# Joining the edge blocks of three attention passes in five parts instead of one

## The chip, the cores and the metric

One NeuronCore of a Trainium2 chip runs the whole kernel. The metric is the device time of one execution in microseconds (us), the median of the runs shown.

## The reference, cut to what matters

A stack of four graph layers on N = 3125 nodes and E = 50000 edges with 128 features: a GCN layer, an edge-attention layer with 8 heads ("attn"), two GAT layers with 3 heads and 1 head ("gat1", "gat2"), and two SAGE layers. The change touches the three attention layers only. Each computes, per head and per destination node,

```python
m = segment_max(logits, dst)
ex = exp(logits - m[dst])
denom = segment_sum(ex, dst)
agg = segment_sum(ex / denom[dst] * rows[src], dst)
```

## The kernel before, in words

The edges are sorted by destination and cut into CH = 392 blocks of 128 edges; GC = 4 blocks are a group (NG = 98), two groups a pair (NPR = 49). An attention pass (`edge_pass`, one function on each engine) walks over the groups with a hand-written software pipeline: `ticks` calls a list of stages once per pair, each with its own lag, so the order inside a list is the order in that engine's queue.

Per group, POOL gathers the source rows with 4 indirect DMAs (L1021) into a ring of RB = 8 slots; before group n it waits for the message multiply of group n-8 (`msg_done`). SP loads the same-destination masks, the breaks and, in attn, the edge attributes and destination rows, each into a ring of four. PE turns attributes (`attr_t`, L1565), multiplies them into edge terms (`edge_terms`, L1573), spreads destination rows over the edges (`dst_rows`, L1584 in attn, L1589 in the GAT passes) and sums the messages per destination (`sums`, L1613). DVE does, in this order per pair: `maxima` (two scans, L2257 and L2263, which need PE's transpose of the logits), `terms` of the even group (attn: L2224 adds the edge terms, L2227 multiplies, L2243 reduces; GAT: L2234, L2247), `difs` (L2270, needs PE's `max_t`, L1604), `terms` of the odd group, and `messages` (L2286) of the two groups before. ACT copies PSUM out (`evac`, L1052), takes the exponentials (L1189) and stores every block's sums to the scratch tensor `ends` (L1167).

Edge terms and destination rows go to two PSUM banks each, by turns, so PE may compute those of group g+1 while DVE still reads those of group g:

```python
                    if g >= 2:
                        pe.wait_ge(kve_done.sem, kve_done.at(p, g, 2))
                    for k in range(GC):
                        i = mm(bank((1, 6)[g % 2])[:, k * D:(k + 1) * D], at_t[:, g % 2, k * P:(k + 1) * P], w_e[:, :],
```

A node's edges can run over a block's edge, so after the last group the blocks are joined: a scan over all 392 blocks for the running maximum, four factors (exponentials of differences), and for the denominators and every 128 columns a scan of the sums. This is the tail of a pass: PE L1626 brings the blocks' maxima together, DVE L2300 to L2316 and ACT L1221 make the factors, PE L1642 spreads them over the partitions, L1659 turns the first and last rows of the blocks (which SP loads back from `ends` by L631), DVE L2328 to L2335 scan, PE L1671 turns back, ACT copies, SP stores (L631), and only then POOL gathers the results (L1030) for the node-wise stage that follows. The tail's chain is serial: each step waits for the one before.

Of the kernel before, what the change touches and what calls it, by code (L numbers as in the profile page):

```python
# [9 lines left out]
ALU = mybir.AluOpType  # L10
# [62 lines left out]
def groups_by(b):  # L73

    return max(0, b - SAME0) * NG // (NB - SAME0)

# [100 lines left out]
def gnn_stack_kernel(nc, out, x, src, dst, edge_attr_64, **w):  # L177
    ctx = ExitStack()
    with ctx:
# [150 lines left out]
        r_rows = place(9700, CQ, QA, wide_w)  # L330
        z_rows = place(11748, CQ, QA, wide_w)
        f_rows = place(13296, CQ, QA, wide_w)
        ex_sb = place(14844, P, 4, CH)
        u_col = place(16412, P, CH)
        s_col = place(16804, P, CH)
        t_col = place(17196, P, H2, CH)
        ex_h = place(18372, H1, 4, CH)
        run_m = place(19940, H1, CH)
        top_m = place(20332, H1, CH)
        u_den = place(20724, H1, CH)  # L340
        s_den = place(21116, H1, CH)
        t_den = place(21508, H1, CH)
# [128 lines left out]
        spread_ps = sem("spread_ps")  # L471
        col_ps, col_ex, col_done, col_back, col_out = (sem(f"col_{k}") for k in ("ps", "ex", "done", "back", "out"))
# [51 lines left out]
        for p in ("gcn",) + PASSES + ("sage1", "sage2"):  # L524
            if p in WEIGHTED:
                chain("s_" + p, ["firsts"] + (["er_in", "er_ps", "er_sb"] if p != "attn" else []))
                chain("x_" + p, ["z_in", "r_out"])
# [71 lines left out]
        cols_of, at_cols = {}, 0  # L599
        for p in PASSES:  # L600
            cols_of[p] = at_cols
            at_cols += col_chunks(p) + 1

        def col_at(p, ch):

            return cols_of[p] + ch + 1

        SPAN_STEPS = 5
        span_of, at_span = {}, 0
        for p in PASSES:  # L610
            span_of[p] = at_span + SPAN_STEPS
            at_span += SPAN_STEPS + 3 * (col_chunks(p) + 1)

        def span_end(p):

            return span_of[p]
# [10 lines left out]
        def _(sp):  # L627
# [151 lines left out]
            def edge_pass(p):  # L779
                c = chains["x_" + p]  # L780
# [39 lines left out]

                for g in range(NG):
# [3 lines left out]
                for g in (NG - 2, NG - 1):  # L825
                    sp.wait_ge(ends_out.of(g), ends_out.at(p, g))
                sp.wait_ge(s_steps, c.at("z_in"))
                v = ends[p][0:EP, :].rearrange("(a t e) c -> t a e c", a=QA, e=P)
                load(z_rows[:, :, 0:W], v[:, :, 0, :])
                load(f_rows[:, :, 0:W], v[:, :, P - 1, :])  # L830
                landed()
                sp.sem_inc(s_steps, 1)
                sp.wait_ge(col_out, col_at(p, col_chunks(p)))
                load(ends[p][EP + P:EP + P + CH, :].rearrange("(a t) c -> t a c", a=QA), r_rows[:, :, 0:W])
                landed()
                sp.sem_inc(s_steps, 1)
# [26 lines left out]
            sp.wait_ge(s_steps, chains["x_gat2"].end)  # L863
# [12 lines left out]
        def _(pool):  # L876
# [130 lines left out]
            def edge_pass(p):  # L1007
# [18 lines left out]
                pool.wait_ge(s_steps, chains["x_" + p].end)  # L1026
# [21 lines left out]
        def _(act):  # L1048
# [111 lines left out]
            def edge_pass(p):  # L1160
# [45 lines left out]

                if p in er_all:
# [5 lines left out]
                if p == "attn":  # L1213
                    ticks([(evac, 2, -4), (keep_max, 1, -1), (attr_sb, 2, 2), (exps, 1, -1), (evac, 2, -3),
                           (attr_sb, 2, 3), (same_f32, 2, 3), (same_f32, 2, 4), (store_ends, 2, -4), (store_ends, 2, -3)])
                else:
                    ticks([(evac, 2, -4), (keep_max, 1, -1), (exps, 1, -1), (evac, 2, -3),
                           (same_f32, 2, 3), (same_f32, 2, 4), (store_ends, 2, -4), (store_ends, 2, -3)])

# [1354 lines left out]
```

## Time and profile before

| | us |
|---|---|
| median of 3 runs (3553.38 to 3568.37) | 3554.34 |
| profiled execution, its own time | 3551.71 |
| its span | 3550.1 |

The page gives PE busy 69% of the span, PE's weight loads 52%, DVE 40%, ACT 27%, POOL 38%; the granted TensorE clock is 0.743 on the mean. The three passes stand in the trace at about 715 to 1444 us (attn), 1571 to 2312 us (gat1) and 2420 to 3128 us (gat2), 98 groups each. No engine is busy all the time, so shares do not tell the bound: it has to be read from who waits for whom.

### The profile page before, as it was taken

Reading aid. Unit: us, or ns where it says so; the run is one execution under the profiler, and the core shown is the slowest. Engines: PE = TensorE matmul, PEld = TensorE weight load, DVE = VectorE, ACT = ScalarE, POOL = GpSimd, SP = SyncE. Lnnn points to the kernel's source line nnn. Section 1 sums busy time; section 2 is a strip of 40 time slices with the busy share of each in tenths; the row PEclk is TensorE's granted clock in tenths of the full one; section 3 lists DMA queues with packets and bytes.
Section 4 is the critical chain, followed back from the end, with each engine's and each line's share of the span. In section 5 each row is a group of like instructions: output and inputs, shape, how many; then the busy total and the mean of one; then the engine's idle time right before and its main releaser. Section 6 shows DMA issues by size and latency. Waiting matters only on the chain.

```text
span 3550.1 us, 36582 instructions
## 1 busy us (share of the span) xinstructions
PE 2464.1 (69%) x12427; PEld 1828.4 (52%) x12427; DVE 1418.4 (40%) x3070; ACT 962.5 (27%) x2050; POOL 1354.0 (38%) x1417
## 2 busy tenths in 40 slices
PE   4999997377666766545677666664565655649998
PEld 3666665256555555333444444443564555526666
DVE  6756555244444455533333333431221212251423
ACT  3422223122222222442333333231221222220202
POOL 3000002645444553375555555045565555320000
PEclk9777788677777787667888888776555555569999
DMA  9388641456666674124555655322344444346362
GB/s 210 115 300 297 234 147 39 139 167 189 175 177 180 177 199 142 26 55 125 169 184 172 189 181 186 107 70 52 88 112 95 106 105 103 94 137 205 116 205 66
DMA packets 518595, 517.78 MB, mean 146 GB/s; under 512 B 154128, under 2 KB 463763, under 8 KB 517227
## 3 DMA queue, kind: packets, MB, share of 16 engines
q1 hardware_dynamic: 310349, 267.24, 24.9%
q0 software_dynamic: 50528, 115.22, 13.3%
q10 hardware_dynamic: 157534, 132.98, 11.9%
q8 instruction: 102, 1.67, 0.2%
q14 instruction: 82, 0.67, 0.1%
HBM read 301.13 MB, written 227.33 MB: 149 GB/s over the span
## 4 chain that ended last, share of the span: by engine, by line
PE 40%; another core or an unknown queue 25%; DVE 12%; issue 12%; ACT 6%; DMA 2%; POOL 1%; ACTq 0%; DVEq 0%; SPq 0%
PE ps L1613 9%; PE ps L1540 8%; PE ps L1434 6%; PE ps L1444 5%; ACT arena L1052 4%; DVE arena L2224 2%; DMA ends_gat<-arena 1%; PE ps L1522 1%; DVE arena L2286 1%; PE ps L1589 1%; PE ps L1573 1%; PE ps L1584 1%; DVE arena L1934 1%; DVE arena L2227 1%
## 5 line engine op out<-in xcount | busy, mean ns | idle before, releaser
L1052 ACT ACTIVATE arena<-ps 128x544 f32<-128x544 f32 (+9 forms) x591 | 485.9, 825 | 1746.1 <-remote 874.5
L1613 PE MATMUL ps<-arena 128*128 128x136 f32 (+2 forms) x2352 | 695.9, 460 | 376.3 <-ACT arena L1052 194.6
L1021 POOL DMA_INDIRECT arena<-t_gat,src_i x784 | 741.9, 946 | 537.1 <-DVE arena L2286 307.8
L1613 PEld LDWEIGHTS ps<-arena 128*128 128x128 f32 x2352 | 479.6, 269 | 516.4 <-issue 425.2
L1021 POOL DMA_INDIRECT arena<-t_attn,src_i x392 | 375.4, 958 | 344.1 <-DVE arena L2286 225.3
L2257 DVE TENSOR_TENSOR_SCAN arena<-arena,ps 64x128 f32<-64x128 f32 (+2 forms) x147 | 60.0, 408 | 803.0 <-remote 714.2
L1540 PE MATMUL ps<-arena 128*128 128x384 bf16 x1850 | 308.2, 331 | 37.6 <-issue 25.1
L1589 PEld LDWEIGHTS ps<-arena 128*128 128x128 f32 x1568 | 288.3, 268 | 45.2 <-issue 22.5
L1589 PE MATMUL ps<-arena 128*128 128x3 f32 (+1 forms) x1568 | 266.6, 292 | 15.7 <-issue 15.7
L1540 PEld LDWEIGHTS ps<-arena 128*128 128x128 bf16 x1850 | 183.1, 99 | 162.4 <-issue 46.0
L2286 DVE TENSOR_TENSOR arena<-arena,ps 128x1536 f32<-128x1536 f32 (+1 forms) x196 | 230.6, 1218 | 38.7 <-ACT arena L1189 30.1
L1444 PE MATMUL ps<-arena 128*128 128x100 bf16 x1176 | 224.4, 364 | 9.4 <-DVE arena L2064 9.2
L1434 PE MATMUL ps<-arena 128*128 128x385 bf16 x925 | 221.0, 413 | 0.0
L984 POOL TENSOR_TENSOR arena<-arena,r_L_gnn_gamma 128x512 f32<-128x512 f32 (+1 forms) x7 | 8.1, 1158 | 533.4 <-ACT arena L1252 533.3
L1444 PEld LDWEIGHTS ps<-arena 128*128 128x128 bf16 x1176 | 169.3, 145 | 58.9 <-DVE arena L2064 12.6
L1573 PE MATMUL ps<-w_e,arena 64*128 64x128 f32 x784 | 148.6, 324 | 59.7 <-issue 59.2
L1604 PE MATMUL ps<-ident,arena 64*128 64x64 f32 (+2 forms) x147 | 40.8, 278 | 201.1 <-DVE arena L2263 164.9
L2270 DVE TENSOR_TENSOR dif<-logit,ps 128x64 f32<-128x64 f32 (+2 forms) x147 | 27.4, 187 | 374.9 <-remote 199.5
L1052 ACT ACTIVATE arena<-same_b 128x512 f32<-128x512 bf16 x294 | 167.7, 619 | 29.6 <-DMA same_b<-same_hbm 28.7
L1573 PEld LDWEIGHTS ps<-w_e,arena 64*128 64x128 f32 x784 | 120.4, 222 | 88.5 <-issue 88.4
L1434 PEld LDWEIGHTS ps<-arena 128*128 128x128 bf16 x925 | 112.2, 121 | 102.9 <-issue 68.9
L1052 ACT ACTIVATE arena<-arena 128x512 bf16<-128x512 f32 (+4 forms) x208 | 64.3, 309 | 346.1 <-DVE arena L2524 247.8
(320 smaller groups left out, 2942.1 us busy)
## 6 DMA issues: line engine op xcount, KB each, us to landing
ends_gat<-arena ACTq DMA_DIRECT2D x98, 774.0 KB
arena<-adj_hbm SPq DMA_DIRECT2D x90, 640.0 KB, 4.2
same_b<-same_hbm SPq DMA_DIRECT2D x294, 128.0 KB
adj_hbm<-arena SPq DMA_DIRECT2D x9, 3200.0 KB, 11.8
ends_attn<-arena ACTq DMA_DIRECT2D x98, 272.0 KB
ends_gat<-arena ACTq DMA_DIRECT2D x98, 258.0 KB
arena<-edst SPq DMA_DIRECT2D x98, 256.0 KB, 4.2
starts_q<-zrow SPq DMA_DIRECT2D x28, 896.0 KB, 6.8
```

The source lines that it names most:

```text
L1021: g.indirect_dma_start(out=row_b[:, n % RB, k, 0:row_tab[p].shape[1]], out_offset=None, in_=row_tab[p], in_offset=bass.IndirectOffsetOnAxi ...
L1052: return a.activation(o, i, ACT.Copy)
L1434: i = mm(bank(4 + n % 4)[:, 0:3 * D + 1], lhs, xs0[:, t, 0:3 * D + 1], start=t == 0, stop=t == NT - 1)
L1444: i = mm(ps[:, at:at + KEYS], hot_e[:, b % 3, :, e], hot_k[:, b % 3, :, e], start=True, stop=True)
L1540: m = mm(bank(ch % 2 * 4 + dl)[:, 0:3 * D], ring[:, u % RING, at:at + P], xs1[:, t, :, :].rearrange("p s c -> p (s c)"), start=t == 0, sto ...
L1573: i = mm(bank((1, 6)[g % 2])[:, k * D:(k + 1) * D], at_t[:, g % 2, k * P:(k + 1) * P], w_e[:, :], start=True, stop=True)
L1589: i = mm(ps[:, at:at + n_er], same_f[:, g % RB, k, :], er_c[:, g * GC + k, 0:n_er], start=True, stop=True)
L1604: nc.tensor.transpose(bank(2)[:, 256:256 + kh], mx[0:kh, i % 2, :], ident[0:kh, 0:kh])\
L1613: i = mm(o, same_f[:, g % RB, k, :], msg[:, g % 4, k * W:(k + 1) * W], start=True, stop=True)
L2224: tt(kv, kv, bc(bank((1, 6)[g % 2]).rearrange("p (k s c) -> p k s c", k=GC, s=1), [P, GC, 2, D]), ALU.add).then_inc(kve_done.sem, 1)
L2257: v.tensor_tensor_scan(fwd[0:kh, s, :], b[:, 0:P], bank(2)[0:kh, 0:P][:, ::-1], -BIG, ALU.add, ALU.max)\
L2286: tt(m[:, :, 0:heads * nc_].rearrange("p k (h c) -> p k h c", h=heads), rows_v, e, ALU.mult).then_inc(msg_done.sem, 1)
```

## The change

The 392 blocks are split in five parts, the first four of 72 blocks (18 groups) and the last of 104. Each of the first four is joined inside the pass, by small steps ("mini") that are put in the tick lists some 7 to 20 groups after the part's last group; the running maximum and the scanned sums are carried from part to part. The last part alone is joined after the last group, by the same chain as before over 104 blocks. `slots_of` fixes at which group's slot each step stands; in a slot of an even group DVE's step comes before `messages`, in one of an odd group after them. Buffers: the part's rows, factors and scans lie in other places of the arena and in a node-stage buffer. A PSUM bank is needed for a part while the groups go on: bank 6 in attn and gat2, bank 1 in gat1. For that, attn's edge terms have bank 1 alone, and gat1's destination rows bank 3 alone; gat2 keeps both of its banks. The `wait` for DVE's use of them goes back one group instead of two. In PE's lists of attn and gat1 `max_t` moves before `edge_terms` and `dst_rows`.

On DVE `tops` is 9 small operations, `mask` is 1 and `join` 7 per chunk of columns, on 72 to 105 columns each. On PE `edges_of` is 16 small products, and it calls `cols_in`, which waits for the two row loads that SP issued (`s_rows`). Not shown of the diff: the semaphore counts and the steps' own waits.

```diff
+PARTS = [(0, 72), (72, 144), (144, 216), (216, 288), (288, CH)]
...
+        def slots_of(p):
...
+            for q in range(QP - 1):
+                s = PARTS[q][1] // GC + 7
+                put(s, "edges", q, 0)
+                put(s + 1, "tops", q, 0)
+                put(s + 2, "exp", q, 0)
+                put(s + 3, "mask", q, 0)
+                put(s + 3, "join", q, 0)
+                for ch in range(1, col_chunks(p) + 1):
+                    put(s + 1 + 3 * ch, "cols", q, ch)
+                    put(s + 2 + 3 * ch, "copy", q, ch)
+                    put(s + 3 + 3 * ch, "join", q, ch)
+                s += 4 + 3 * col_chunks(p)
+                put(s, "back", q, 0)
+                put(s + 1, "rows", q, 0)
...
@@ SP, edge_pass @@
+                def rows_for(q):
+                    b0, b1 = PARTS[q]
+                    g1 = b1 // GC
+                    for g in (g1 - 2, g1 - 1):
+                        sp.wait_ge(ends_out.of(g), ends_out.at(p, g))
+                    if part_at(p, q) > 1:
+                        sp.wait_ge(col_ps, col_at(p, q, 0) - 1)
+                    sp.dma_start(z_rows[0:b1 - b0, 0:W], v_ends[b0:b1, 0, :]).then_inc(s_rows, 16)
+                    sp.dma_start(f_rows[0:b1 - b0, 0:W], v_ends[b0:b1, P - 1, :]).then_inc(s_rows, 16)
...
+                def sums_out(q):
+                    b0, b1 = PARTS[q]
+                    sp.wait_ge(col_out, back_at(p, q, col_chunks(p)))
+                    sp.dma_start(ends[p][EP + P + b0:EP + P + b1, :], r_rows[0:b1 - b0, 0:W]).then_inc(s_rout, 16)
...
+                rows_at = {PARTS[q][1] // GC + 10: q for q in range(QP - 1)}
+                out_at = {PARTS[q][1] // GC + 19 + 3 * col_chunks(p): q for q in range(QP - 1)}
                 for g in range(NG):
                     if g % 2 == 0:
                         load_breaks(g // 2)
                     load_group(g)
+                    if g in out_at:
+                        sums_out(out_at[g])
+                    if g in rows_at:
+                        rows_for(rows_at[g])
...
@@ ACT, edge_pass, gat1 and gat2 (attn the same with attr_sb) @@
+                    ticks([(evac, 2, -4), (keep_max, 1, -1), (exps, 1, -1), (mini, 2, 0), (evac, 2, -3),
+                           (same_f32, 2, 3), (same_f32, 2, 4), (store_ends, 2, -4), (store_ends, 2, -3),
+                           (mini, 2, 1)])
...
@@ PE, edge_pass @@
                 def edge_terms(g):
                     pe.wait_ge(attr_sb_done.sem, attr_sb_done.at(p, g))
-                    if g >= 2:
-                        pe.wait_ge(kve_done.sem, kve_done.at(p, g, 2))
+                    if g >= 1:
+                        pe.wait_ge(kve_done.sem, kve_done.at(p, g, 1))
                     for k in range(GC):
-                        i = mm(bank((1, 6)[g % 2])[:, k * D:(k + 1) * D], at_t[:, g % 2, k * P:(k + 1) * P], w_e[:, :],
+                        i = mm(bank(1)[:, k * D:(k + 1) * D], at_t[:, g % 2, k * P:(k + 1) * P], w_e[:, :],
...
                 def dst_rows(g):
                     pe.wait_ge(same_f_done.sem, same_f_done.at(p, g))
-                    if g >= 2:
-                        pe.wait_ge(prod_done.sem, prod_done.at(p, g, 2))
+                    back = 1 if p == "gat1" else 2
+                    if g >= back:
+                        pe.wait_ge(prod_done.sem, prod_done.at(p, g, back))
...
-                            at = (3, 1)[g % 2] * BANK + k * n_er
+                            at = (3, 3 if p == "gat1" else 1)[g % 2] * BANK + k * n_er
...
+                def edges_of(q, ch=0):
+                    b0, b1 = PARTS[q]
+                    i0, i1 = b0 // PB, b1 // PB
+                    pe.wait_ge(kept_done.sem, kept_done.at(p, i1 - 1))
...
+                    for s, t in enumerate((o.last[:, 1:], o.first)):
+                        for k in range(PB):
+                            i = mm(t[:, k::PB], ident[0:kh, k * heads:(k + 1) * heads], edge_m[0:kh, i0:i1, s],
+                                   start=True, stop=True)
+                    i.then_inc(edge_m_ps, 1)
+                    if q < QP - 1:
+                        cols_in(q, 0)
...
                 if p == "attn":
-                    ticks([(logit_t, 1, -1), (sums, 2, -4), (attr_t, 2, 2), (edge_terms, 2, 1), (dst_rows, 2, 1),
-                           (max_t, 1, -1), (sums, 2, -3), (attr_t, 2, 3), (edge_terms, 2, 2), (dst_rows, 2, 2)])
+                    ticks([(logit_t, 1, -1), (sums, 2, -4), (attr_t, 2, 2), (max_t, 1, -1), (edge_terms, 2, 1),
+                           (dst_rows, 2, 1), (sums, 2, -3), (attr_t, 2, 3), (mini, 2, 0), (edge_terms, 2, 2),
+                           (dst_rows, 2, 2), (mini, 2, 1)])
+                elif p == "gat2":
+                    ticks([(logit_t, 1, -1), (sums, 2, -4), (dst_rows, 2, 1), (max_t, 1, -1), (sums, 2, -3),
+                           (mini, 2, 0), (dst_rows, 2, 2), (mini, 2, 1)])
                 else:
-                    ticks([(logit_t, 1, -1), (sums, 2, -4), (dst_rows, 2, 1), (max_t, 1, -1), (sums, 2, -3),
-                           (dst_rows, 2, 2)])
-
+                    ticks([(logit_t, 1, -1), (sums, 2, -4), (max_t, 1, -1), (dst_rows, 2, 1), (sums, 2, -3),
+                           (mini, 2, 0), (dst_rows, 2, 2), (mini, 2, 1)])
...
@@ DVE, edge_pass @@
-                ticks([(maxima, 1, -1), (terms, 2, 0), (difs, 1, -1), (terms, 2, 1), (messages, 2, -2), (messages, 2, -1)])
+                ticks([(maxima, 1, -1), (terms, 2, 0), (difs, 1, -1), (terms, 2, 1), (mini, 2, 0), (messages, 2, -2),
+                       (messages, 2, -1), (mini, 2, 1)])
+                tops(QP - 1)
+                mask(QP - 1)
                 for ch in range(col_chunks(p) + 1):
+                    join(QP - 1, ch)
```

## Rows read from the trace of the kernel before

**Rows 1.** Busy time by stretch, the three passes' loops; then PEclk, DMA share, GB/s.
```profile
715.00:1415.00 700.00, 493.53 (x2766) 413.11 (x2765) 346.26 (x528) 180.22 (x429) 345.01 (x360) 0.75 0.63 176
1571.00:2269.00 698.00, 441.05 (x1680) 287.50 (x1681) 240.65 (x441) 216.42 (x393) 371.45 (x393) 0.81 0.54 167
2420.00:3099.00 679.00, 372.96 (x1709) 359.97 (x1710) 141.13 (x466) 136.50 (x394) 382.35 (x404) 0.51 0.41 97
```
**Rows 2.** Waits, attn's loop, then gat1's: us in total, times, longest.
```profile
POOL arena L1021 <- DVE arena L2286: 225.3, 27, 20.0
...
POOL arena L1021 <- DVE arena L2286: 165.7, 51, 10.6
```
**Rows 3.** Timeline of POOL in attn: end of one run of gathers, start of the next.
```profile
1009.77 0.95 POOL L1021 DMA_INDIRECT arena<-t_attn,src_i  x1 [0.30 <-issue]
1021.50 0.94 POOL L1021 DMA_INDIRECT arena<-t_attn,src_i  x1 [10.78 <-DVE arena L2286]
```
**Rows 4.** Timeline of attn between those two: DVE and PE.
```profile
1013.71 2.07 PE L1584 MATMUL ps<-arena 128*128 128x128 f32 x8 [0.34 <-issue]
...
1013.86 0.41 DVE L2257 TENSOR_TENSOR_SCAN arena<-arena,ps 64x128 f32<-64x128 f32 x1 [14.63 <-remote]
...
1014.65 1.19 DVE L2224 TENSOR_TENSOR arena<-arena,ps 128x1024 f32<-128x1024 f32 x1
...
1017.48 1.22 DVE L2224 TENSOR_TENSOR arena<-arena,ps 128x1024 f32<-128x1024 f32 x1
...
1018.71 1.16 PE L1573 MATMUL ps<-w_e,arena 64*128 64x128 f32 x8
...
1019.79 1.16 PE L1584 MATMUL ps<-arena 128*128 128x128 f32 x8
```
**Rows 5.** Busy time by stretch, the same place: columns as in Rows 1.
```profile
1013.80:1018.30 4.50, 4.50 (x19) 4.07 (x20) 4.26 (x7) 1.74 (x6) 0.00 (x0) 0.50 0.64 179
1018.50:1032.00 13.50, 10.34 (x78) 8.81 (x76) 9.98 (x16) 3.93 (x10) 8.07 (x9) 1.00 0.73 208
```
**Rows 6.** Timeline of gat1 at such a place.
```profile
1836.40 0.41 DVE L2257 TENSOR_TENSOR_SCAN arena<-arena,ps 24x128 f32<-24x128 f32 x1 [11.49 <-remote]
...
1837.70 0.17 DVE L2234 TENSOR_TENSOR z_b<-arena,ps 128x12 f32<-128x12 f32 x1
...
1840.90 0.95 POOL L1021 DMA_INDIRECT arena<-t_gat,src_i  x1 [7.20 <-DVE arena L2286]
...
1842.21 0.95 PE L1589 MATMUL ps<-arena 128*128 128x3 f32 x8
```
**Rows 7.** Timeline of gat2 at such a place: DVE, then POOL.
```profile
2569.00 0.41 DVE L2257 TENSOR_TENSOR_SCAN arena<-arena,ps 8x128 f32<-8x128 f32 x1 [15.12 <-remote]
...
2572.29 0.94 POOL L1021 DMA_INDIRECT arena<-t_gat,src_i  x1 [6.35 <-DVE arena L2286]
```
**Rows 8.** Timeline of attn's tail: its first step, SP's store, the gather that follows.
```profile
1414.94 2.78 PE L1626 MATMUL ps<-arena,ident 64*8 64x49 f32 x32
...
1441.08 0.31 SPq L631 DMA_DIRECT2D ends_attn<-arena  x1
1443.90 0.95 POOL L1030 DMA_INDIRECT arena<-ends_attn,end_i  x1 [63.74 <-SPq L836]
```
**Rows 9.** Groups by form in attn's tail: busy us, mean ns.
```profile
L2331 DVE TENSOR_TENSOR_SCAN arena<-arena 128x392 f32<-128x392 f32 x1 | 1.0, 974 | 0.0
...
L2306 DVE COPY arena<-span_m 8x1 f32<-8x1 f32 x1 | 0.1, 131 | 0.0
```
**Rows 10.** Chain of gat1's tail, its first step and its end; then gat2's.
```profile
2269.00 1.54 PE ps L1626 x32
...
2307.98 3.75 DMA ends_gat<-arena
2311.77 0.26 issue
...
3099.63 2.71 PE ps L1626 x32
...
3128.51 0.94 POOL arena L1030
```

More of the change, by code:

```diff
@@ L75, in groups_by @@
     return max(0, b - SAME0) * NG // (NB - SAME0)
+PARTS = [(0, 72), (72, 144), (144, 216), (216, 288), (288, CH)]
+QP = len(PARTS)
+PW = max(b - a for a, b in PARTS)
+assert all(a % PB == 0 for a, b in PARTS) and PW <= P
 PIECE = [(c, t, t + HI) for c in range(NC - 1) for t in range(0, NT, HI)] + [(NC - 1, 0, 13), (NC - 1, 13, NT)]
@@ L824, in edge_pass @@
                     load_group(g)
[L825 to L836, printed above, removed]
+                    if g in out_at:
+                        sums_out(out_at[g])
+                    if g in rows_at:
+                        rows_for(rows_at[g])
+                for q in range(QP - 1):
+                    if PARTS[q][1] // GC + 19 + 3 * col_chunks(p) >= NG:
+                        sums_out(q)
+                rows_for(QP - 1)
+                sums_out(QP - 1)
             for j in range(NJ):
@@ new lines, in spread_of @@
+                def spread_of(q, ch):
+                    n = PARTS[q][1] - PARTS[q][0]
+                    if ch == 1:
+                        pe.wait_ge(span_dve, span_at(p, q) + SPAN_STEPS)
+                        if q == QP - 1:
+                            pe.wait_ge(evac_done.sem, evac_done.at(p, NG - 1))
+                    elif q == QP - 1:
+                        pe.wait_ge(col_ex, ex_at(p, q, ch) - 1)
+                    for e in range(4):
+                        lhs = spread[:, :] if p == "attn" else bc(ident[0:heads, ch - 1:ch], [heads, P])
+                        i = mm(Psum(p, q).ex[e], lhs, ex_h[0:heads, e, 0:n + 1], start=True, stop=True)
+                    i.then_inc(spread_ps, 1)
@@ new lines, in cols_in @@
+                def cols_in(q, ch):
+                    n = PARTS[q][1] - PARTS[q][0]
+                    o = Psum(p, q)
+                    if ch == 0:
+                        if q == QP - 1:
+                            pe.wait_ge(span_set, part_at(p, q))
+                        pe.wait_ge(s_rows, 32 * part_at(p, q))
+                    elif ch >= 2 or q < QP - 1:
+                        pe.wait_ge(col_done, col_at(p, q, ch - 1))
+                    for t, z in ((z_rows, o.den_z if ch == 0 else o.z), (f_rows, o.den_f if ch == 0 else o.f)):
+                        if ch == 0:
+                            src_v = t[0:n, heads * cols:W]
+                        elif p == "attn":
+                            src_v = t[0:n, 0:heads * cols]
+                        else:
+                            src_v = t[0:n, (ch - 1) * cols:ch * cols]
+                        i = nc.tensor.transpose(z, src_v, ident[0:n, 0:n])
+                    i.then_inc(col_ps, 1)
+                    if 0 < ch and q < QP - 1:
+                        spread_of(q, ch)
```

356 lines of the change are left out of this document (207 added, 149 removed).

## The prediction

> **What bounds the kernel now.** I read first the busy time by stretch for the three loops [rows 1]. Each takes 679 to 700 us for 98 groups, and no engine is busy throughout: PE 441 and POOL 371 of 698 us in gat1, PE 494 and POOL 345 of 700 us in attn. So the loops are bound by handing over, not by an engine, and the waits have to say whose. In attn POOL waited 225.3 us in 27 waits for the message multiply L2286; in gat1 165.7 us, in more and shorter waits [rows 2]. POOL's timeline shows the form: gathers come in runs, most of 16 (four groups), one every 1.25 us, so 20 us a run; after the run that ended at 1010.7 POOL idled 10.78 us and began again at 1021.50 [rows 3]. What ends that pause is read on DVE: it sat idle 14.63 us, resumed with the scan L2257 at 1013.86, and POOL began again 7.6 us later, when the tick's messages were out [rows 4]. In gat1 the resume is at 1836.40 and POOL's start at 1840.90, 4.5 us later, after a pause of 7.20 [rows 6]; in gat2 2569.00, 2572.29, 3.3 us and 6.35 [rows 7]. The pause less that stretch is 3.1, 2.7 and 3.1 us: the same in all three. So a period is a run of gathers (20 us), a lag of about 3 us, and then **the stretch from DVE's resume to the first messages**. What holds DVE until the run is over the rows don't say (the wait has no releaser in them), but whatever is done during the run is free, and whatever lengthens the stretch after it is paid in every period. 98 groups by four make 24.5 periods; some are shorter or overlap, so I count 225.3 / 10.8 = 21 for attn and 165.7 / 7.2 = 23 for gat1.
>
> **Part 1, the tails.** From PE's first join step to POOL's first gather, attn's tail takes 1443.90 - 1414.94 = 29.0 us [rows 8], gat1's 2311.77 + 0.26 - 2269.00 = 43.0, gat2's 3128.51 - 3099.63 = 28.9 [rows 10]. All of it is on the path, since POOL gathers the results only after it. After the change the chain is the same over 104 blocks instead of 392. What doesn't shrink: SP's store to the gather's start, 2.8 us in attn [rows 8], 4.1 in gat1 [rows 10]; and the fixed part of each operation, 0.13 us by a copy of one column [rows 9], about 30 operations in attn and 45 in gat1, so 4 and 6 us; and 1 to 2 us of handing over. The rest scales with 104/392 = 0.27: a scan falls from 0.974 us [rows 9] to about 0.36 (0.41 for 128 columns [rows 4]). Attn: 29.0 - 2.8 - 4 - 1 = 21.2, to 5.7, so 13.5 are left and 15.5 saved. Gat2 the same. Gat1: 43.0 - 4.1 - 6 - 2 = 31, to 8.4, so 20.5 left and 22.5 saved. In attn and gat2 SP's rows of the last part come about when the shorter chain wants them, so I take 1 us off: **52 us saved**, bounds 40 (fixed costs twice as large) and 58. The price of PE's 32 tiny products in it (13 columns instead of 49) is the least certain; by the rows it is between 0.27 of 2.78 us [rows 8] and all of it, and I took 0.27 of the variable part. The Trainium skill, TensorE: Matmul & The Clock Gate, Part 1, says start to start never drops below about 25 ns however few the columns; by that estimate the 32 would take at least 0.8 us a pass. No row here has 13 columns.
>
> **Part 2, attn's edge terms in one bank.** Now PE makes edge terms and destination rows of the odd group during the stall: its L1584 ends about when DVE resumes [rows 4], so DVE goes from the even group's L2224 (1014.65, 1.19 us) over two multiplies and `difs` straight to the odd group's L2224 at 1017.48. After the change `edge_terms` of the odd group must wait for the even group's L2224, that is until 1015.85, and destination rows stand behind it in PE's queue. Two prices for these 16 matmul instructions: 1.16 + 1.16 us as at 1018.71 and 1019.79, or twice 2.07 as L1584 at 1013.71 [rows 4]. With 0.15 us for the semaphore the odd L2224 begins at 1018.3 (+0.8) or 1020.1 (+2.7). The granted clock decides: it was 0.50 (1.2 GHz) from 1013.8 to 1018.3, after the stall, and 1.00 (2.4 GHz) from 1018.5 on [rows 5]. So the first falls wholly and the second mostly on 1.2 GHz: I take +2.0 us. Queued behind PE's new wait are `sums` and the even group's work; behind DVE's are the messages, POOL's restart and so the next run. In the tick inside the run the same wait falls at 2.4 GHz, where `difs` waited for `max_t` anyway, and `max_t` now comes earlier: nothing. 21 x 2.0 = **+42 us**, bounds 0 (if the period gives way elsewhere) and 24.5 x 2.7 = 66.
>
> The Trainium skill, same page, Part 1, says that the throttled clock is the default and activity releases it; by that rule PE, left waiting longer in the stall, comes back at the low clock, and the term would be 21 x 2.7 = 57 rather than the 17 of the high clock. The trace agrees as far as 0.50 after the stall [rows 5] goes.
>
> **Part 3, gat1's destination rows in one bank.** The same, smaller. Now the odd L2234 runs at 1837.70, 1.3 us after the resume; after the change its 8 products (0.95 us at 1842.21 [rows 6]; about 1.7 by attn's ratio of 2.07 to 1.16 [rows 4]) start only after the even L2234 and `max_t`, which end at about 1837.6. So it begins at 1838.7 to 1839.4, +1.0 to +1.7. DVE waited there for the exponentials before the messages, which takes 0.3 of it back: I take +1.0. 23 x 1.0 = **+23 us**, bounds 0 and 24.5 x 1.4 = 34.
>
> **Part 4, the steps inside the passes.** PE (16 products, transposes, spreads), ACT (an exponential, copies) and SP (three small DMAs a part) have room during the stalls; none of theirs stands between resume and messages in their queues. DVE's do when their slot is even: at 0.2 us an operation (between 0.13 [rows 9] and 0.41 [rows 4]) `tops` 1.8 and `mask` with the first `join` 1.6 us, in gat1 one more `join` 1.4. Each meets the stretch that counts in one tick of two: 4 parts x 3.4 / 2 = 7 us in attn and gat2, 4 x 4.8 / 2 = 10 in gat1: 24 us. Some of it falls where DVE waits: **+20 us**, bounds 8 and 35. If the stalls' cover went, it would be about 80 us of PE, ACT and DVE work more. SP's new waits come after its loads for the group, four groups ahead of use, and I cost them at nothing.
>
> **The sum.** -52 + 42 + 23 + 20 = +33 us against the profiled execution's own 3551.7 us, which is 2.6 below the median of 3554.3; on the median, **3587 us**. About 0.5% (18 us) is what a measurement of this kernel can tell from no change.
>
> **Rivals.**
> A, the tails come off and the loops don't notice: the wait moves into the 14 us of stall, because the tick in which the run ends shifts so that PE's new wait falls inside the run. For it: the stall is long and POOL's restart needs only one tick. Against it: three passes with stretches of 7.6, 4.5 and 3.3 us have the same 3 us of lag, so the stretch is paid in full each time. It gives 3554 - 52 + 12 = 3514 us. Chance 0.27.
> B, in between: the high clock after the stall, or half of the periods hit: -52 + 17 + 12 + 20 = -3, 3551 us. Chance 0.13.
> C, slower by another wait: PE's `edges` slot calls `cols_in`, which waits for rows that SP asks for in the same pair or the pair before; if they land only when the run of gathers is over, PE stands before the next logit transposes, and POOL's next run starts a tick late. 12 parts at up to 7.6 us [rows 4] are 91 us on top of nothing else lost: 3554 - 52 + 33 + 91 = 3626 us. It decides from the point where a row load takes longer than one tick, about 7 us. Chance 0.10, beside 0.50 for my forecast.
> D, the change doesn't do what it says: the last part's chain is no shorter, because the rows that SP loads after the last store set its pace. The store, the load and their landing are some 7 us, the shorter chain up to that point about 6: it costs 1 to 2 us a pass and is in the bounds.
>
> **Range and chances.** A has faster; B lies within 0.5%; the forecast and C are slower, though the forecast's lower fifth isn't by over 0.5%. Faster 0.28, same 0.16, slower 0.56. The range takes in A with its costs, 3508, and reaches up to the forecast's upper bounds short of all at once, 3640. The forecast's own range is 3560 to 3640.
>
> **What would show it.** The tails at about 14, 21 and 14 us; in attn the odd L2224 after a resume some 5 us after the even one instead of 2.8, with L1573 and L1584 between them; POOL's pauses 12 to 13 us in attn, 8 in gat1, unchanged in gat2 but for some; runs still of 16. Wrong if attn's loop stays at 700 us, or if a row wait (`s_rows`) stands in PE's list.

## The result, and the profile after

The changed kernel takes 3619.73 us (median of 4 runs, 3600.88 to 3624.94) where the kernel before took 3556.52 on the same chip: ratio 1.017, 95% interval 1.0136 to 1.0204, that is +60 us (48 to 73). Forecast were +33 us, 3587, with a range to 3640. The profiled execution has a span of 3623.0 us.

The page of the changed kernel: the span, three engines, then the gathers and the messages.

```profile
span 3623.0 us, 38294 instructions
...
PE 2501.5 (69%) x12995; PEld 1875.2 (52%) x12995; DVE 1455.3 (40%) x3430; ACT 965.6 (27%) x2106; POOL 1347.4 (37%) x1417
...
L1109 POOL DMA_INDIRECT arena<-t_gat,src_i x784 | 740.0, 944 | 593.1 <-DVE arena L2419 364.2
...
L1109 POOL DMA_INDIRECT arena<-t_attn,src_i x392 | 371.4, 947 | 421.8 <-DVE arena L2419 303.8
```

PE is as busy as before, 69%. What grew is POOL's wait for the message multiply (now L2419), in attn from 225.3 us [rows 2] to 303.8. POOL's timeline tells where: it gives a pass three marks, its first gather of rows, its last, and the first gather of results. Before:

```profile
660.97 0.98 POOL L1021 DMA_INDIRECT arena<-t_attn,src_i  x1 [0.30 <-issue]
1379.20 0.95 POOL L1021 DMA_INDIRECT arena<-t_attn,src_i  x1 [0.30 <-issue]
1571.68 0.97 POOL L1021 DMA_INDIRECT arena<-t_gat,src_i  x1 [0.30 <-issue]
2222.16 0.94 POOL L1021 DMA_INDIRECT arena<-t_gat,src_i  x1 [0.30 <-issue]
2445.17 0.97 POOL L1021 DMA_INDIRECT arena<-t_gat,src_i  x1 [0.31 <-issue]
3071.22 0.94 POOL L1021 DMA_INDIRECT arena<-t_gat,src_i  x1 [0.30 <-issue]
```

After, the same with the gather of results (L1118):

```profile
662.86 0.97 POOL L1109 DMA_INDIRECT arena<-t_attn,src_i  x1 [0.30 <-issue]
1454.62 1.05 POOL L1109 DMA_INDIRECT arena<-t_attn,src_i  x1 [0.30 <-issue]
1503.73 0.94 POOL L1118 DMA_INDIRECT arena<-ends_attn,end_i  x1 [48.06 <-DMA ends_attn<-arena]
1630.62 0.97 POOL L1109 DMA_INDIRECT arena<-t_gat,src_i  x1 [0.30 <-issue]
2321.96 0.95 POOL L1109 DMA_INDIRECT arena<-t_gat,src_i  x1 [0.30 <-issue]
2388.72 0.94 POOL L1118 DMA_INDIRECT arena<-ends_gat,end_i  x1 [65.82 <-DMA ends_gat<-arena]
2520.90 0.97 POOL L1109 DMA_INDIRECT arena<-t_gat,src_i  x1 [0.30 <-issue]
3160.13 0.95 POOL L1109 DMA_INDIRECT arena<-t_gat,src_i  x1 [0.30 <-issue]
3203.67 1.00 POOL L1118 DMA_INDIRECT arena<-ends_gat,end_i  x1 [42.59 <-DMA ends_gat<-arena]
```

From the first gather of rows to the last ("the loop" from here on) the passes take 718, 650 and 626 us before, 792, 691 and 639 after: +74, +41, +13, in sum +128. From the last gather of rows to the gather of results ("the tail") it is 64.7, 89.9 and 57.3 before [rows 8, 10 give the ends], 49.1, 66.8 and 43.5 after: -53 together. 128 - 53 = 75, and the two profiled spans are 73 us apart, so little else moved. (By the medians it is +60; the profiled execution is the longest of the four.) The joins did leave the tails, and by as much as forecast. What went wrong is in the loops, forecast at +85.

The tail of attn itself, with the rows that answer to [rows 8], and the first step of gat2's tail:

```profile
1490.95 0.96 PE L1734 MATMUL ps<-arena,ident 64*8 64x13 f32 x32
...
1501.90 0.30 SPq L908 DMA_DIRECT2D ends_attn<-arena  x1
1503.73 0.94 POOL L1118 DMA_INDIRECT arena<-ends_attn,end_i  x1 [48.06 <-DMA ends_attn<-arena]
...
3190.35 0.95 PE L1734 MATMUL ps<-arena,ident 8*1 8x13 f32 x32
```

From PE's first step to POOL's gather attn's tail takes 12.8 us, where 13.5 stood in the sum; the 32 records of the tiny products took 0.96 us. (A product of this kernel stands in the trace as two records: x32 is 16 products.)

**How the loops changed.** In attn, runs of 16 gathers turned into runs of 8 for most of the pass. (Here and below a pause of under 2 us doesn't end a run. Of the 360 gathers behind the first 32, 32 stood in runs of 8 before and 216 after.) The timeline of attn, one such period:

```profile
1010.43 0.94 POOL L1109 DMA_INDIRECT arena<-t_attn,src_i  x1 [5.83 <-DVE arena L2419]
...
1012.87 1.19 DVE L2357 TENSOR_TENSOR arena<-arena,ps 128x1024 f32<-128x1024 f32 x1
...
1014.81 1.30 PE L1681 MATMUL ps<-w_e,arena 64*128 64x128 f32 x8
...
1019.18 0.95 POOL L1109 DMA_INDIRECT arena<-t_attn,src_i  x1 [0.30 <-issue]
1021.92 1.22 DVE L2357 TENSOR_TENSOR arena<-arena,ps 128x1024 f32<-128x1024 f32 x1 [6.29 <-remote]
...
1023.29 2.04 PE L1681 MATMUL ps<-w_e,arena 64*128 64x128 f32 x8 [4.72 <-DVE arena L2357]
...
1025.93 0.94 POOL L1109 DMA_INDIRECT arena<-t_attn,src_i  x1 [5.81 <-DVE arena L2419]
```

The even group's L2357 (the addition of the edge terms, L2224 before) runs at 1012.87. PE's edge terms of the odd group (L1681) had to wait for it and stand in PE's list at 1014.81, 4.4 us into the run of gathers, but the odd L2357, which needs them, starts only at 1021.92, 2.7 us after the last gather was issued. In the kernel before they stand 0.9 us into the run:

```profile
990.91 0.94 POOL L1021 DMA_INDIRECT arena<-t_attn,src_i  x1 [10.47 <-DVE arena L2286]
...
991.78 1.16 PE L1573 MATMUL ps<-w_e,arena 64*128 64x128 f32 x8
...
995.37 1.22 DVE L2224 TENSOR_TENSOR arena<-arena,ps 128x1024 f32<-128x1024 f32 x1
```

The odd L2224 follows at 995.37, within the run, the whole second tick gets through, and 16 gathers are freed. Now a period is 15.5 us for 8 gathers, 31.0 for 16 instead of 30.55, and where a run of 16 still occurs it mostly takes 32 to 37 us. The slower pace is more than the 0.45 us between 31.0 and 30.55: on the mean of the loop behind its first 32 gathers, 16 of them took 29.3 us before and 32.5 after.

In gat2, whose banks are untouched, all but four of the periods are like before (24.9 to 26.5 us for 16 gathers). One of those that are not:

```profile
2832.20 0.94 POOL L1109 DMA_INDIRECT arena<-t_gat,src_i  x1 [6.42 <-DVE arena L2419]
...
2833.53 0.95 PE L1734 MATMUL ps<-arena,ident 8*1 8x9 f32 x32
2834.41 0.40 PE L1769 MATMUL ps<-ident,arena 72*1 72x72 f32 x2
2834.60 0.42 PE L1706 MATMUL ps<-ident,logit 128*8 128x128 f32 x1
...
2840.95 0.94 POOL L1109 DMA_INDIRECT arena<-t_gat,src_i  x1 [0.30 <-issue]
2842.19 0.41 DVE L2390 TENSOR_TENSOR_SCAN arena<-arena,ps 8x128 f32<-8x128 f32 x1 [10.15 <-issue]
```

Here a part's `edges` (L1734) stands ahead of the logit transpose L1706, which the scan L2390 needs. By the records it all fits into 1.1 us, yet the scan that needs L1706 starts 7.2 us after the end of it, when the run, 8 gathers long now, is over; 15.4 us for 8 gathers instead of 13. In gat1 one part shows more of it:

```profile
1961.48 0.69 PE L1734 MATMUL ps<-arena,ident 24*3 24x9 f32 x22
1963.19 0.22 PE L1734 MATMUL ps<-arena,ident 24*3 24x9 f32 x3 [1.01 <-issue]
1963.91 0.17 PE L1734 MATMUL ps<-arena,ident 24*3 24x9 f32 x1 [0.49 <-issue]
1965.33 0.17 PE L1734 MATMUL ps<-arena,ident 24*3 24x9 f32 x1 [1.25 <-issue]
...
1973.06 0.40 PE L1769 MATMUL ps<-ident,arena 72*3 72x72 f32 x2 [1.23 <-issue]
```

The first 22 records go in 0.7 us and the last ten take about 10: PE waits for nothing that the profile shows and mostly advances by one record in 0.7 us or a multiple of it, while POOL gathers.

### The profile page after: what moved, and what is told of

It reads as the page before. It is cut to its first block and busy times, and to the rows that moved or that the text cites. A ratio compares the mean times of both kernels' runs of the same rounds, so it can differ in the third digit from the quotient of the medians.

```text
span 3623.0 us, 38294 instructions
## 1 busy us (share of the span) xinstructions
PE 2501.5 (69%) x12995; PEld 1875.2 (52%) x12995; DVE 1455.3 (40%) x3430; ACT 965.6 (27%) x2106; POOL 1347.4 (37%) x1417
## 3 DMA queue, kind: packets, MB, share of 16 engines
q0 software_dynamic: 50528, 115.22, 12.8%
## 5 line engine op out<-in xcount | busy, mean ns | idle before, releaser
L1140 ACT ACTIVATE arena<-ps 128x544 f32<-128x544 f32 (+7 forms) x610 | 479.2, 794 | 1893.7 <-remote 882.5
L1722 PEld LDWEIGHTS ps<-arena 128*128 128x128 f32 x2352 | 486.3, 271 | 367.8 <-issue 290.7
L1109 POOL DMA_INDIRECT arena<-t_attn,src_i x392 | 371.4, 947 | 421.8 <-DVE arena L2419 303.8
L2390 DVE TENSOR_TENSOR_SCAN arena<-arena,ps 64x128 f32<-64x128 f32 (+2 forms) x147 | 60.0, 408 | 776.8 <-remote 635.7
L1698 PEld LDWEIGHTS ps<-arena 128*128 128x128 f32 x1568 | 292.7, 275 | 61.8 <-issue 52.1
L1698 PE MATMUL ps<-arena 128*128 128x3 f32 (+1 forms) x1568 | 282.4, 302 | 43.6 <-issue 20.6
L1681 PE MATMUL ps<-w_e,arena 64*128 64x128 f32 x784 | 150.8, 349 | 185.9 <-DVE arena L2357 168.0
L2419 DVE TENSOR_TENSOR arena<-arena,ps 128x1536 f32<-128x1536 f32 (+1 forms) x196 | 230.1, 1215 | 17.5 <-ACT arena L1277 11.9
L1681 PEld LDWEIGHTS ps<-w_e,arena 64*128 64x128 f32 x784 | 131.5, 251 | 202.0 <-ACT arena L1140 117.3
L2357 DVE TENSOR_TENSOR arena<-arena,ps 128x1024 f32<-128x1024 f32 x98 | 118.0, 1204 | 265.4 <-remote 219.1
L1713 PEld LDWEIGHTS ps<-ident,arena 64*128 64x128 f32 (+2 forms) x147 | 23.2, 158 | 358.9 <-DVE arena L2396 302.3
```

Of the source, the lines that this page charges most:

```text
L1109: g.indirect_dma_start(out=row_b[:, n % RB, k, 0:row_tab[p].shape[1]], out_offset=None, in_=row_tab[p], in_offset=bass.IndirectOffsetOnAxi ...
L1140: return a.activation(o, i, ACT.Copy)
L1681: i = mm(bank(1)[:, k * D:(k + 1) * D], at_t[:, g % 2, k * P:(k + 1) * P], w_e[:, :], start=True, stop=True)
L1698: i = mm(ps[:, at:at + n_er], same_f[:, g % RB, k, :], er_c[:, g * GC + k, 0:n_er], start=True, stop=True)
L1713: nc.tensor.transpose(bank(2)[:, 256:256 + kh], mx[0:kh, i % 2, :], ident[0:kh, 0:kh])\
L1722: i = mm(o, same_f[:, g % RB, k, :], msg[:, g % 4, k * W:(k + 1) * W], start=True, stop=True)
```

## The experiments

All ratios are to the kernel before on the same chip. The loops come from one profiled execution each and scatter: gat1's, left as it was, took 650, 659 and 659 us in three kernels, and attn's with one and the same code 708 and 690 (e2, e7). 10 us between two loops of gat1, or 20 of attn, are therefore no finding. gat2's is steadier: left as it was it took 626 to 630 us in all six kernels that have it so (e1, e2, e3, e7, e12 and the one before). The ratios carry the verdicts. A difference of two ratios is less sure than either: between two kernels of four or five runs it is good to some 10 to 20 us.

| kernel | ratio (95%) | loops: attn, gat1, gat2 |
|---|---|---|
| before | 1 | 718, 650, 626 |
| changed | 1.0170 (1.0136 to 1.0204) | 792, 691, 639 |
| e1 shared banks, no parts | 1.0118 (1.0099 to 1.0137) | 745, 666, 627 |
| e2 attn order; gat1 bank | one run | 708, 665, 627 |
| e3 attn bank; gat1 order | one run | 747, 662, 630 |
| e12 attn bank and order | 1.0078 (1.0052 to 1.0103) | 755, 659, 630 |
| e7 attn order | 0.9972 (0.9951 to 0.9992) | 690, 659, 628 |
| e4 changed, DVE's steps behind messages | 1.0136 (1.0106 to 1.0165) | 770, 685, 639 |
| e10 e4, `edges` spread | 1.0080 (1.0053 to 1.0108) | 756, 672, 627 |
| e9 e1 + 16 products x 12 | 1.0186 (1.0137 to 1.0234) | 762, 669, 632 |
| e5 e1 + 32 products x 12 | 1.0284 (1.0263 to 1.0305) | 758, 693, 642 |
| e6 e1 + 32 products x 144 | one run | 1005, 813, 752 |
| e8 e6, other place | one run | 948, 814, 761 |
| e11 e6, gat2 without gathers | one run | 1002, 810, - |

**The banks.** e1 is the kernel before with these lines of the change:

```diff
-                    if g >= 2:
-                        pe.wait_ge(kve_done.sem, kve_done.at(p, g, 2))
+                    if g >= 1:
+                        pe.wait_ge(kve_done.sem, kve_done.at(p, g, 1))
...
-                    if g >= 2:
-                        pe.wait_ge(prod_done.sem, prod_done.at(p, g, 2))
+                    back = 1 if p == "gat1" else 2
+                    if g >= back:
+                        pe.wait_ge(prod_done.sem, prod_done.at(p, g, back))
```

with the one bank that belongs to each, and PE's lists of attn and gat1 with max_t ahead of edge terms and destination rows. 

> The kernel before, with the changed PE lists and the shared banks of attn and gat1 but no parts: the joins stay in the tails. The loops are measured from the first gather of rows to the last; before they took 718, 650 and 626 us (attn, gat1, gat2), in the changed kernel 792, 691 and 639. Theory 1, the prediction's: the banks cost most of it, +42 in attn (760) and +23 in gat1 (673), 3557 + 65 = 3622 us in all. Theory 2, from the trace of the changed kernel: gat1's undisturbed periods still take 27.1 us, so its bank costs 0 to 5 (650 to 655), and attn's gathers now come in runs of 8 every 15.5 us, 31.0 for 16 where 30.5 stood, so +12 (730); in all about 3572 us. The rest of the added time would then be the steps'. gat2 and the tails stay under both.

Measured: 1.0118, +42 us (35 to 49), loops 745, 666, 627. That lies between the theories, by the loops (+27 and +16) as by the ratio. attn's runs are of 8 every 15.5 us, as in the changed kernel, and there are no parts here: the bank or the order makes them. The other 18 us of the +60 are then parts: +71 of steps less 53 of tails, both good to some 15 us. Two single runs took each pass apart:

> The kernel before, attn with only max_t moved ahead (two banks kept), gat1 with only its destination rows in one bank (order kept). Theory 1: attn at most 718, the wait needs the bank; gat1 673 or more, since max_t now stands behind the waiting destination rows. Theory 2: attn 718 with runs of 16 as before, gat1 650 to 655. If attn's runs turn to 8 here, the order and not the bank is what changes them.

> The kernel before, attn with only the edge terms in one bank (order kept), gat1 with only max_t moved ahead. Theory 1: attn 760 or more, for max_t stands behind the waiting edge terms and difs waits for it in every tick. Theory 2: attn between 730 and 760, runs of 8 if the bank makes them; gat1 650 or a little less.

e2: attn 708 with the order alone; gat1 665. e3: attn 747 with the bank alone. Of the 360 gathers behind the first 32, 104 stand in runs of 8 with the order alone (e7 below has the same) and 248 with the bank alone, where the kernel before has 32 and e1 280. So the bank halves most of the runs, but the order by itself halves some as well, and its loop is none the longer: a run of 8 takes 14.3 us in e2 and 15.1 in e3. The length of a run is not the price; what a tick takes is. Theory 1's fear that max_t behind the waiting edge terms makes it worse doesn't show (747 beside 745). Theory 1's 760 was too much here, and 747 lies within theory 2's 730 to 760. gat1 took 662 with the order alone, within the scatter of its loop.

e12 is attn's half of e1, and gat1 as before. 

> The kernel before with attn's part of the shared banks alone: edge terms in one bank and max_t ahead of them; gat1 is untouched. Both together cost 38 us. By the loops of the profiled runs 27 of 42 us are attn's, so 3556 + 25 = 3581 us, and gat1's bank costs some 13; by the prediction's terms attn's is 42, 3598 us.

Measured: 1.0078, +28 us (18 to 37); gat1's bank and order then have some 14 us, by a difference of two ratios that is good to some 12. As expected from the loops, and below the 42 of the sum.

e7 moves one entry of attn's list and keeps both banks:

```diff
-                    ticks([(logit_t, 1, -1), (sums, 2, -4), (attr_t, 2, 2), (edge_terms, 2, 1), (dst_rows, 2, 1),
-                           (max_t, 1, -1), (sums, 2, -3), (attr_t, 2, 3), (edge_terms, 2, 2), (dst_rows, 2, 2)])
+                    ticks([(logit_t, 1, -1), (sums, 2, -4), (attr_t, 2, 2), (max_t, 1, -1), (edge_terms, 2, 1),
+                           (dst_rows, 2, 1), (sums, 2, -3), (attr_t, 2, 3), (edge_terms, 2, 2), (dst_rows, 2, 2)])
```

> The kernel before with one thing of the change alone: in attn's PE list max_t stands ahead of edge terms and destination rows, two banks kept, no parts. In a run that also changed gat1, attn's loop fell from 718 to 708 us so. If that is the order's doing, this kernel takes 3547 us, 0.3% less than the kernel before; if it was one execution's scatter, 3556.

Measured: 3552.21 us beside 3563.33, 0.9972 (0.9951 to 0.9992): 10 us less (3 to 17). It is the fastest kernel of this study, faster than both. POOL's waits in its attn:

```profile
POOL arena L1021 <- DVE arena L2286: 187.9, 28, 19.4
```

187.9 us where [rows 2] had 225.3. (The profiled execution is the fastest of the eleven; e2, with the same code in attn, has 205.5.) So against a good order the shared bank of attn costs 28 + 10 = 38 us, good to some 12.

**DVE's steps.** e4 changes `slots_of` alone (and the group at which SP stores a part's sums): every DVE step stands on an odd slot, behind the messages, the chunks four groups apart. The steps of ACT, and PE's behind `edges`, move to other slots with them.

```diff
-                put(s + 1, "tops", q, 0)
-                put(s + 2, "exp", q, 0)
-                put(s + 3, "mask", q, 0)
-                put(s + 3, "join", q, 0)
+                put(s + 2, "tops", q, 0)
+                put(s + 3, "exp", q, 0)
+                put(s + 4, "mask", q, 0)
+                put(s + 4, "join", q, 0)
```

> The changed kernel with every step of DVE in the slot behind the messages (tops two groups after edges, joins four groups apart instead of three), nothing left out. Theory 1: the steps cost 24 us in all, so the loops give back at most that: attn 785, gat1 681, gat2 632. Theory 2: the steps in front of the messages are what disturbs the periods: gat1 655 to 660, gat2 628, attn 745 or less, in all about 3550 us. Theory 3: it is PE's steps, its waits or the loads that disturb: all loops as in the changed kernel, 792, 691, 639.

Measured: 1.0136 against the changed kernel's 1.0170, 12 us back, by the medians 20. gat2's loop stays at 639 and gat1's is 685. Theory 2, 3550 us, falls: most of the steps' price is elsewhere. The 12 us fit theory 1's size for DVE, but the two intervals overlap (1.0106 to 1.0165, 1.0136 to 1.0204), so that theory 3, nothing back, is not ruled out.

**PE's products.** e5 adds to e1, at the four slots of `edges` in each pass, products on constants that nothing reads:

```diff
+                def spare(i):
+                    if i in (12, 21, 30, 39):
+                        for k in range(32):
+                            mm(bank(1 if p == "gat1" else 6)[0:8, k * 9:(k + 1) * 9], ident[0:128, 0:8],
+                               ident[0:128, 0:9], start=True, stop=True)
```

> The kernel with the shared banks alone (the first experiment), and in each pass four times 32 tiny products on PE, 9 columns each, in the tick and place of the parts' first step (ahead of the logit transposes); nothing of ACT, DVE, POOL or SP. They stand for a part's `edges`, which in the changed kernel took 0.8 to 0.95 us at its best. Its loops were 745, 666 and 627 us. Linear theory: PE's work counts as long as it is, 4 x 0.9 us, so at most 4 us a pass. Window theory, from gat2 of the changed kernel: a run of gathers is 16 long only where the second tick's transpose of the logits gets in right after the run starts; a PE step ahead of it makes the run 8 long, so 4 times some 2.5 us, gat2 637, attn and gat1 up to 10 more. If gat2 stays at 627 to 631, the in-pass steps' price there is not that of PE's products.

What this expectation says of the size is off by two: 32 products are 64 records, twice what `edges` has. Measured: 1.0284, +59 us over e1, 4.9 us for each of the 12 (4.1 to 5.8), where 64 records at the best pace are 1.6 us. Both theories had less, the linear one by far. With `range(16)`, the true size of `edges`:

> The kernel with the shared banks alone, and at the four slots of each pass 16 products of 9 columns on PE, as many as a part's `edges` has (32 records in the trace; the earlier run had 32 products, 64 records, twice a part's). That run cost 67 us over the shared banks alone, 5.6 us each. Theory A, the cost goes by the number of products: 2.8 us each, so 12 x 2.8 = 33 us, 3628 us in all, and `edges` is the largest single part of the 77 us that the parts' steps cost in the changed kernel. Theory B, the first 32 records go fast (0.8 us in the records of that run) and only those behind them wait: at most 12 x 0.9 = 11 us, 3605 us, and the steps' cost lies elsewhere.

Measured: 1.0186, +24 us over e1, 2.0 each. Theory A's 33 us are within the error; theory B's 3605 us lie under the fastest of the four runs, 3613. But the interval is wide, 1.0137 to 1.0234: with that of e1 it leaves 5 to 43 us, and theory B's 11 are in it. That 16 tiny products in a tick cost some 2 us, and not their 0.8 of records, rests on e5 as much, where twice as many cost 4.9.

e6 has the 32 products in 48 of 49 ticks, e8 the same behind max_t.

> The same 32 tiny products in nearly every tick (48 of 49) of all three passes, ahead of the logit transposes. Linear theory: 48 x 0.9 = 43 us a pass at most, less what the runs of gathers hide: gat2 at most 670, runs still 16 long. Window theory: all of gat2's runs fall to 8 gathers, 15.4 us each instead of 26.1 for 16, so 627 + 24 x 4.7 = 740; gat1 likewise about 750; attn, whose runs are 8 long already, at most 745 + 43 = 788.

> The products of the run with 32 of them in every tick, moved: behind max_t instead of ahead of the logit transposes, same number. Linear theory: same loops as there. Window theory: the place decides; in gat2 the products lie after the second tick's max_t, which is the last that the run's second half needs, so runs stay 16 long and gat2 takes 627 to 650 us where it takes 740 with the products ahead of the transposes.

In e6 gat2's runs fell to 8 gathers in 16.0 us for all but three, in e8 they stayed 16 with 32.6 us (some with a pause of 1.0 us in the middle). The window theory had the length of the runs right in both, and gat2's time in e6 (740 forecast, 752 measured); e8 refutes its reason, with 761 us where 627 to 650 stood. So in gat2 the place of PE's work decides how long a run is, and its amount decides the time: for 64 records in each tick 2.6 to 3.1 us in gat2 and gat1, 4.2 to 5.4 in attn. The linear theory was right for the GAT passes that the place doesn't matter, and had the price, 0.9 us, at a third. In attn the place counts too: 1005 us in e6, 948 in e8.

The timeline of PE in e6, gat2, during a run of gathers:

```profile
3142.13 0.81 PE L1620 MATMUL ps<-ident 128*8 128x9 f32 x26
...
3143.32 0.17 PE L1620 MATMUL ps<-ident 128*8 128x9 f32 x1 [0.38 <-issue]
...
3149.05 0.17 PE L1620 MATMUL ps<-ident 128*8 128x9 f32 x1 [1.26 <-issue]
...
3156.13 0.17 PE L1620 MATMUL ps<-ident 128*8 128x9 f32 x1 [1.21 <-issue]
3157.53 0.75 PE L1620 MATMUL ps<-ident 128*8 128x9 f32 x24 [1.23 <-issue]
```

26 records in 0.8 us, then 14 in 14.6 us; the run's last gather was issued at 3153.4, and from 3157.5 the other 24 go in 0.75 us. This is one of the three long runs. In most ticks of this pass the first stretch is longer and the steps are larger:

```profile
3181.51 1.73 PE L1620 MATMUL ps<-ident 128*8 128x9 f32 x51
3184.41 0.28 PE L1620 MATMUL ps<-ident 128*8 128x9 f32 x5 [1.17 <-issue]
```

e11 takes the gathers away, in gat2 alone, and loads neighbouring rows in their place:

```diff
+                    if p == "gat2" and g >= RB:
...
+                        sp.wait_ge(msg_done.sem, msg_done.at(p, g, RB))
+                        for k in range(GC):
+                            sp.dma_start(row_b[:, g % RB, k, 0:row_tab[p].shape[1]], row_tab[p][k * P:(k + 1) * P, :])\
+                              .then_inc(rows_h[g % RB], 16)
...
-                for n in range(NG):
+                for n in range(RB if p == "gat2" else NG):
```

> The kernel with 32 products in nearly every tick, whose loop took 752 us in gat2; in gat2 alone the gathers of rows by POOL are replaced from the ninth group on by plain loads of 128 neighbouring rows, of the same size, on SP's queue (other rows than the reference's, so gat2 and what follows compute on wrong rows). Theory A, it is the run of gathers that slows PE: the 64 records of a tick take no more than 1.7 us everywhere, the long stalls of DVE go, and the loop falls below 500 us. Theory B, PE itself or its supply of instructions is slow: records 0.7 us and more apart remain, and the loop stays above 600 us.

The products in gat2, all records of the line (min/median/max ns, first and last start), of e6 and then of e11:

```profile
L1620 PE MATMUL ps<-ident x2816: 173/174/183, 2960.1 to 3640.6; 128*8 128x9 f32 x188
its engine sat idle before it (us, times) until:
  issue: 334.9, 387
```

```profile
L1630 PE MATMUL ps<-ident x2752: 170/173/183, 2961.4 to 3305.7; 128*8 128x9 f32 x197
its engine sat idle before it (us, times) until:
```

PE's timeline in one tick of e11:

```profile
3110.16 1.76 PE L1630 MATMUL ps<-ident 128*8 128x9 f32 x64
3111.85 0.38 PE L1608 MATMUL ps<-ident,logit 128*8 128x128 f32 x1
```

With gathers PE idled 334.9 us in 387 stops before these records, without them never; a tick's 64 go in 1.76 us, the long stalls of DVE are gone, and gat2 takes 473 us from its first gather to the gather of results instead of 811. Theory A. That POOL's gathers slow PE is shown; the same bytes by plain loads on SP's queue do not. Nor is it the mere load on the DMA engines: their busy share is 0.61, at 146 GB/s, from 2943 to 3375 us of e11, and 0.35 at 82 GB/s in gat2 of e6. By which way the gathers do it is open. e11 changed three things together, POOL's work on the gathers, the queue that the rows come by, and scattered rows for neighbouring ones, and no run takes them apart.

e10 is e4 with the 16 products of `edges` in attn and gat2 as four times four, two groups apart; the later steps of these parts stand six groups later:

```diff
                 put(s, "edges", q, 0)
+                if p != "gat1":
+                    for part in (1, 2, 3):
+                        put(s + 2 * part, "edges", q, part)
+                    s += 6
```

> The changed kernel with DVE's steps behind the messages (3599 us), and in attn and gat2 the 16 products of `edges` spread over four pairs, four products in each. Theory A, every product costs wherever it stands: 3599 us, loops of attn and gat2 stay at 770 and 639. Theory B, the cost comes where too many stand in one tick, so that the next transpose of the logits comes late: the eight parts of the two passes give back about 2.8 us each, 3577 us, gat2's loop about 628.

Measured: 1.0080 against 1.0136, 20 us back (5 to 35), for eight parts 2.5 each, about what e9 found them to cost; 3580.56 us. Theory B. The clearest sign is gat2's steady loop: 627 us, that of the kernel before, where the changed kernel and e4 have 639, and its tail stays at 43. There the joining inside the pass costs nothing that shows. attn's loop gave back 13 us, and its tail took 7 of them; gat1, where e10 changes nothing, is 13 us shorter by scatter. Products cost where many stand in one tick, not each by itself.

## Why the prediction was right, and where it was not

The direction held, and the kernel is slower by more than forecast: +60 beside +33. The sum came that near partly by luck: the banks were put 23 us too high and the steps inside the passes 51 too low. Term by term:

- **The tails: -52 forecast, -53 measured** (15.6, 23.1 and 13.8 us by pass, where 15.5, 22.5 and 15.5 less 1 stood). The fixed part by operation, the scaled rest and SP's rows were the right model. Its least certain price, the 32 records, came out at 0.96 us. The Trainium skill (TensorE: Matmul & The Clock Gate, Part 1) has at least about 25 ns from start to start. The trace agrees: 0.96 us less the last record's 0.17 are 0.8 us for 31 steps.
- **attn's edge terms in one bank: +42 forecast, +28 measured** with the order, 38 without its help. The wait is the one named. Which of the two prices, at 1.2 or 2.4 GHz, held for it no run separates. One step that failed is "nothing" for the tick inside the run, where `max_t` now comes earlier: moved ahead by itself, with two banks kept, it gives 10 us back. The other is the way: not a longer stretch in runs of 16, but the odd edge terms caught by the run, with the odd addition 9.1 us after the even one in the period shown, where about 5 were forecast.
- **gat1's destination rows: +23 forecast, about +14 measured** (the difference of two ratios, good to some 12 us).
- **The steps inside the passes: +20 forecast, +71 measured** (60 - 42 + 53, good to some 15). This is where the missing 27 us come from, and more, since the banks were put too high. The sentence that failed is that PE has "room during the stalls". The stall of DVE was taken for free time of PE. But PE hardly gets on while gathers run (e6; in e11, without them, it does), and what is given to PE there delays the next logit transpose. That DVE's stall in the kernel before is this same thing is the likely reading; no run takes the gathers out of that kernel. `edges`, costed at nothing, is some 24 us of the 71 (e9; 2.5 us a part in e10, and e5 with twice the products). DVE's steps ahead of the messages are 12 by e4, within the 8 to 35 given for them, but not clear of noise. For the other 35 (PE's transposes and spreads of the columns, ACT, SP) no run was made; that those of PE follow the same rule is argued, not shown.
- **Rival A** (the loops don't notice) falls with attn's 792 us; so does B. **C**, a wait of PE for the part's rows, did not occur: L1769, the first to need them, has no wait for a DMA in any of the three loops, and follows L1734 at once where PE isn't slowed, as at 2834.41. A loss by PE being late for the logit transposes was right in C, its cause was not. Its time of 3626 us, close to the measured one, is no sign for it: the sum has 33 us for the other costs, which the prediction puts at 42 + 23 + 20 = 85, and with these C gives 3678. **D** falls: the tails are short.
- **What would show it**: tails at 14, 21 and 14 us: 12.8, 21.6 and 13.3. Runs still of 16: wrong in attn. POOL's pauses of 12 to 13 us there: 5.8 after most runs of 8, 11 to 15 after those of 16. Pauses of 8 us in gat1: 7.4 to 9.0 after most runs of 16. gat2 unchanged but for some: right, and the few were the clue.

The "lag of about 3 us" [rows 3, 4] may be the same sign seen too small: PE's work of the run, done only once the gathers end.

## What to carry to other kernels

Before work is moved into another engine's stall, ask what causes the stall: here the engine that seemed to have room was the one held up, and work hidden behind it cost two and a half to three times its records. Spread such work in small pieces over many rounds (in gat2 four products at a time cost nothing that shows, where sixteen cost 2 to 3 us), and look at an instruction's consumer, not at its own record, to see when it was really done. A second buffer that lets one engine run ahead may be worth more than the tail that its space could shorten: attn's bank was worth some 38 us, its shorter tail 16.

## What the hardware showed that was not expected

While POOL's indirect gathers run, PE issues a first 20 to 50 records at full pace (all 64 only where POOL pauses, as from 3121.22 and 3132.50 in e6) and then one to five in 0.7, 1.4 or 2.0 us, with no wait in the profile: 14 records in 14.6 us in e6, and for some 4 us more after the last gather is issued; none of it in e11's gat2, where plain loads move the rows.

It isn't an effect of the profiler alone, for the executions of e5 that weren't profiled take as long (3661 to 3665 us) as the one that was (3660). DVE and ACT go on working in a run, as L2357 at 1012.87 does at its usual 1.2 us, until they need something of PE. Often they then start long after PE's record has ended: L2390 at 2842.19, 7.2 us behind its producer. Whether PE's work is really done that late, or its signal or DVE is held up as well, the traces don't show.

The Trainium skill (SBUF — State Buffer, Who interferes with whom) says of SBUF's ports that "PE and ACT never wait on anyone". The runs here don't show that PE waits for a port, so they don't speak against it there; but PE did wait, 334.9 us in e6's gat2, and the sentence can't be taken as a promise that nothing on another engine holds PE up.

All this means that a run of gathers of 20 us is no cover for PE work. Two things were not tried, as each needs a kernel of its own: gat2's parts of e10 together with e7's order, and the gathers in smaller packs.
